# Attention and mixture-of-experts layer: another order for the first units of a step (output projection before the second maxima, two maxima before the second half of the weighted sums)

## The reference

```
scores = einsum('bhqd,bhkd->bhqk', q, k) * (1.0 / sqrt(HD))
attn   = softmax(scores * causal - (1.0 - causal) * NEG)
out    = einsum('bhqk,bhkd->bhqd', attn, v) -> b, t, d
a      = layernorm(out @ w_proj + b_proj + xn) * ln_gamma + ln_beta
f      = sum over the top 2 experts e of prob_e * (gelu(xn @ W1[e] + b1[e]) @ W2[e] + b2[e])
result = x + a + f
```

## Time and profile before

| | us |
|---|---|
| median of 3 runs (835.06 to 838.79) | 837.65 |
| the profiled execution, its own time | 838.32 |
| its span, first to last instruction | 836.6 |
| TensorE busy | 698.7 (84%) |
| VectorE busy | 653.4 (78%) |
| GpSimd busy | 557.4 (67%) |
| ScalarE busy | 544.8 (65%) |

### The profile page before, as it was taken

How to read it: one execution, slowest core, us unless ns; L and a number is a source line. 1 busy time by engine, 2 the same in 40 slices (tenths; PEclk the granted TensorE clock), 3 DMA queues, 4 the chain that set the end, 5 groups by cost and what they waited for, 6 DMA issues and landing times.

```text
span 836.6 us, 25028 instructions
## 1 busy us (share of the span) xinstructions
PE 698.7 (84%) x7876; PEld 518.2 (62%) x7878; DVE 653.4 (78%) x1550; ACT 544.8 (65%) x1107; POOL 557.4 (67%) x611
## 2 busy tenths in 40 slices
PE   2766989999999999999988878659999999999800
PEld 1543556666666666666656555338988889888700
DVE  5877978888978787878888887637878888888644
ACT  4812646666666666666756656538989999999700
POOL 8521758888877777777887786616766677667700
PEclk9987989999999999999999999869999999999955
DMA  9691323232322232223243333102222222222189
GB/s 271 230 312 59 94 68 100 89 102 89 101 90 100 91 100 91 99 92 107 84 148 120 111 107 93 28 14 73 87 83 80 86 87 82 86 77 90 49 277 333
DMA packets 113313, 93.66 MB, mean 112 GB/s; under 512 B 16618, under 2 KB 97650, under 8 KB 113268
## 3 DMA queue, kind: packets, MB, share of 16 engines
q1 hardware_dynamic: 95508, 70.26, 26.9%
q0 software_dynamic: 8704, 18.17, 6.1%
q10 hardware_dynamic: 9056, 4.66, 1.9%
HBM read 43.85 MB, written 48.93 MB: 111 GB/s over the span
## 4 chain that ended last, share of the span: by engine, by line
PE 60%; DVE 11%; ACT 7%; issue 7%; DMA 6%; POOL 6%; SPq 2%; ACTq 0%; POOLq 0%; DVEq 0%
PE wide L1323 11%; PE bank_head L1212 9%; PE bank_head L1314 5%; PE bank_maxB L1314 5%; PE wide L1177 5%; PE bank_maxA L1191 5%; DVE shift L966 4%; DMA xn_rows<-parts_dram 3%; PE bank_maxB L1191 3%; PE bank_maxA L1195 3%; PE wide L1181 3%; PE bank_misc L1237 3%; DMA pieces_f<-in_w 3%; POOL probs L601 2%; PE bank_maxB L1195 2%
## 5 line engine op out<-in xcount | busy, mean ns | idle before, releaser
L653 POOL DMA_INDIRECT parts_dram<-o_T,dest x144 | 161.3, 1120 | 75.9 <-issue 48.5
L601 POOL TENSOR_SCALAR_AFFINE_SELECT probs<-probs 128x512 f32<-128x512 f32 (+1 forms) x192 | 152.3, 805 | 83.1 <-ACT probs L687 81.0
L687 ACT ACTIVATE probs<-wide 128x1024 f32<-128x1024 f32 x192 | 185.4, 1023 | 31.1 <-PE wide L1177 18.9
L966 DVE TENSOR_REDUCE shift<-bank_maxA 128x2 f32<-128x512 f32 (+1 forms) x192 | 132.3, 689 | 52.4 <-PE bank_maxA L1195 48.7
L592 POOL DMA_INDIRECT x_slots<-xn_rows,slot_i x128 | 131.3, 1026 | 38.9 <-issue 37.5
L966 DVE TENSOR_REDUCE shift<-bank_maxB 128x2 f32<-128x512 f32 (+1 forms) x192 | 131.6, 685 | 5.4 <-PE bank_maxB L1195 1.3
L731 ACT ACTIVATE probs<-wide,b_all 128x256 f32<-128x256 f32 x288 | 121.5, 478 | 16.6 <-PE wide L1323 10.9
L1212 PE MATMUL bank_head<-probs,v_aug 128*32 128x256 f32 (+1 forms) x2048 | 99.6, 336 | 27.5 <-DVE x L992 22.9
L1323 PE MATMUL wide<-xgT_raw,xnT 128*128 128x256 f16 x864 | 109.3, 277 | 6.5 <-DVE xgT_raw L1073 6.5
L1212 PEld LDWEIGHTS bank_head<-probs,v_aug 128*32 128x32 f32 x2048 | 60.3, 112 | 72.3 <-issue 35.0
L1056 DVE TENSOR_TENSOR probs<-probs 128x512 f16<-128x512 f32 x144 | 99.7, 693 | 5.5 <-ACT probs L737 1.1
(11 more groups left out here) (178 smaller groups left out, 1253.3 us busy)
## 6 DMA issues: line engine op xcount, KB each, us to landing
qk_rows<-split SPq DMA_DIRECT2D x32, 512.0 KB, 3.0
x_slots<-fill SPq DMA_DIRECT2D x16, 598.5 KB, 7.8
fill<-x_slots SPq DMA_DIRECT2D x72, 133.0 KB
q_diag<-qk_rows SPq DMA_DIRECT2D x256, 32.0 KB, 1.8
k_cat<-qk_rows SPq DMA_DIRECT2D x64, 128.0 KB, 2.1
xn_rows<-parts_dram SPq DMA_DIRECT2D x8, 1024.0 KB, 11.7
x_all<-in_x SPq DMA_DIRECT2D x8, 512.0 KB, 7.5
pieces_f<-in_w SPq DMA_DIRECT2D x8, 512.0 KB, 4.0
```

What stands on the lines that cost most here:

```text
L601: pool.affine_select(out=part, in_=part, compare_op=ALU.is_ge, fill=0.0, base=0, pattern=[[0, n], [1, P]], channel_multiplier=-1).then_inc ...
L653: pool.indirect_dma_start(out=parts_dram, out_offset=bass.IndirectOffsetOnAxis(ap=dest[:, of, t:t + 1].bitcast(U32), axis=0), in_=y[:, of ...
L687: act.activation(probs[:, u, :], ps[:, :], ACT.Exp, scale=SCALE).then_inc(empty, 1)
L966: V.tensor_reduce(dst, ps[:, :].rearrange("p (j k) -> p j k", j=nh), axis=AX.X, op=ALU.max, negate=True).then_inc(empty, 1)
```

## The change

Two moves in the list USES. The row of proj goes one place forward, ahead of m1. The rows of m2 and m3 go ahead of o1. The order of units within each buffer stays as it was.

```diff
         USES = [
-            ("maxA", "m0", MAXIMA), ("maxB", "m1", MAXIMA), ("head", "proj", LAST),
+            ("maxA", "m0", MAXIMA), ("head", "proj", LAST), ("maxB", "m1", MAXIMA),
             ("misc", "qk", PROJECT),
-            ("head", "o1", FINISH), ("maxA", "m2", MAXIMA), ("maxB", "m3", MAXIMA),
+            ("maxA", "m2", MAXIMA), ("maxB", "m3", MAXIMA), ("head", "o1", FINISH),
             ("misc", "v", MAXIMA), ("maxA", "m4", MAXIMA), ("wide0", "s0", SOFT),
```

## The result

The changed kernel takes 858.26 us (median of 4 runs, 856.63 to 859.95) where the kernel before, run beside it, takes 836.44 us: a ratio of 1.0255, 95% interval 1.0229 to 1.0282. It is slower by some 22 us. The profiled execution of the changed kernel took 856.63 us (its span is 854.9 us, that of before 836.6), so the two traces that are compared here differ by 18.3 us.

A forecast was written before the change was run, and what follows sets the result against it. TensorE was taken to bound the loop, busy 13.38 of 14.00 us a step. Loop 13.0 and tail 3.3 us on the profiled 838.32 made 854.6 us, or 854 against the median; range 846 to 861.

The forecast's parts named there:

- The walk through a loop step: One loop step followed in the new order on the old clock: 0.43 to 0.81 us longer, 0.65 taken.
- the long v: TensorE's v ahead of m4 taken at its full 0.50 us instead of 0.34, so m4 starts at 309.82.
- (b): VectorE in the loop: addition and statistics go ahead of the maximum of m1; maxB is released 1.6 to 1.8 us later.
- (c): TensorE in the loop: m3, now ahead of o1, waits for maxB; TensorE idles about 1.1 us with o1 behind.
- The loop term: Loop steps 4 to 23: 20 x 0.65 = 13.0 us longer, bounds 8.6 and 16.2.
- step (e): Written-out steps 24 to 32: two pay 0.65 us in full, seven 0.28 each; together 3.3 us, bounds 0.9 and 5.9.
- The rival that was priced at 2%: TensorE's clock falls from 2.4 to 1.2 GHz; paid in nine tail steps, 13 us more, 867; chance 0.02.
- o1 did not fill m3's gap: Rival on TensorE in the loop: o1 runs while m3 waits, -0.3 us a step, about 831; chance 0.03.
- the larger loss: Loop: ScalarE's copy of o1 keeps its 0.6 us lag, exponentials start late; up to 0.4 us a step, 861; chance 0.08.
- VectorE's statistics did not shrink: Rival in the loop: VectorE's 1.51 us between addition and split shrinks below 0.6, m1's maximum not late; about 823; chance 0.02.
- nothing hid the loss: Rival in the loop: ScalarE or GpSimd already sets the step's length, so no change; 838 to 842; chance 0.04.

The follow-up runs named there:

- e3: Changed kernel with TensorE keeping the changed list and VectorE given the old order (maximum of m1 ahead of addition and statistics): 835.35 us.
- e4: Kernel before with TensorE's old list kept, VectorE alone taking the addition and statistics ahead of the maximum of m1: 834.25 us.
- e5: Changed kernel with the maximum of m1 put between addition and statistics on VectorE, TensorE's order unchanged: 833.41 us.
- e7: Kernel before with VectorE's split of a piece of expert weights (line 1035) done twice in a row in the written-out steps: 847.42 us.
- e9: Changed kernel with VectorE's split of a piece of expert weights moved from ahead of the addition to behind the maximum of m5: 854.27 us.
- e2: Kernel before with only the second move, m2 and m3 ahead of o1, the projection staying behind m1: 830.11 us.
- e1: Kernel before with only the first move, the projection ahead of m1 on TensorE and VectorE, o1 staying ahead of m2 and m3: 833.17 us.
- e10: e2 with VectorE's split of a piece of expert weights moved behind the maximum of m5: 835.29 us.
- e6: Changed kernel with VectorE's split of a piece moved from ahead of the addition to the end of the step in which ScalarE rounded it: 853.56 us.
- e8: e2 with VectorE's split of a piece moved to the end of the step in which ScalarE rounded it: 834.76 us.

## Why the prediction was right, and where it was not

**The walk through a loop step held at every point.** Measured from the end of m0's mask (304.28 in the earlier trace rows, 311.04 in the changed kernel):

| | forecast | measured |
|---|---|---|
| addition starts | 0.69 to 0.91 | 0.89 |
| maximum of m1 over | 2.88 to 3.10 | 2.98 |
| m3 starts | 2.94 to 3.16 | 3.04 |
| m4 starts | 5.16 to 5.38 (5.54 with the long v) | 5.37 |

m4 stood at 4.73 before, so the step loses 0.64 us there, and 0.62 from start to start (14.62 against 14.00); 0.65 was taken. That no later work gives it back held too. That the cause is the one of steps (b) and (c) is shown by e3, e4 and e5: without the statistics ahead of the maximum, or with o1 ahead of m3, nothing is lost.

**The loop term** was 13.0 us and came out at 11.4 between the two traces. Of these, steps 6 to 23 give 11.6 us; steps 4 and 5 give nothing: they take 19.21 and 14.70 us in the changed kernel, 19.45 and 14.68 in the kernel before. It is not shown that the order costs nothing there, since in both traces a stretch at half clock stands in step 4. The kernel before has one from 106.0 to 112.9 us, the changed kernel from 108.2 to 111.6. e7, whose loop is that of the kernel before, waits just as long in step 4 and has no such stretch:

```profile
107.31 2.79 PE L1212 MATMUL bank_head<-probs,v_aug 128*32 128x256 f32 x32 [3.57 <-DVE x L992]
```

```profile
106.55 1.51 PE L1215 MATMUL bank_head<-probs,v_aug 128*32 128x256 f32 x32 [3.58 <-DVE x L993]
```

(The kernel before, then e7. The 3.57 us are the longest wait in the earlier trace rows.) In e7 steps 4 and 5 take 17.01 and 14.21 us, and against e7's loop, 283.2 us, the changed one is 13.9 us longer. So the forecast lies between what two executions of the old loop give, and the term is right within what step 4 does by itself; that "20 x 0.65" came so near is owed in part to chance.

**The tail term, step (e), was mis-sized: 3.3 us with bounds of 0.9 and 5.9, measured 9.2.** Step by step, with the steps that have a half-clock stretch in the changed kernel in bold:

| step | 24 | 25 | 26 | 27 | 28 | 29 | 30 | 31 | 32 |
|---|---|---|---|---|---|---|---|---|---|
| before | 14.43 | 14.85 | 15.42 | 15.64 | 15.48 | 15.77 | 16.62 | 14.85 | 15.87 |
| after | 14.58 | 15.67 | 15.66 | **17.13** | **17.14** | **17.29** | **17.12** | 15.52 | 18.02 |

Where neither half clock nor a long transfer came in, the steps went about as forecast: 25 and 31, the two in which the chain was to go through TensorE, pay 0.82 and 0.67 us (0.65 forecast), 24 and 26 pay 0.15 and 0.24 (0.28 forecast). The two things that step (e) did not have are the rest.

The four steps with a stretch pay 5.2 us. What a stretch costs can be read in three ways: 1.38 us in e7; 1.55 us in the changed kernel itself, whose four steps with one take 17.17 us in the mean and steps 25, 26 and 31, with the same wait and none, 15.62; and 0.92 us against e9, where steps 28 to 30 have no stretch, but wait for ScalarE instead (16.26 us in the mean against 17.18). By these the four stretches are 3.7 to 6.2 us of the 9.2 (an estimate). Step 32 has 2.15 us, exactly what its piece's transfer took longer, 6.52 us against 4.37 in the kernel before. Why that one transfer took 6.52 us is open. In the other kernels a transfer that leads the chain takes 3.85 to 6.09 us, so it is not shown to come from the change.

Step (e) also took m3's wait as 2.2 us, where it is 1.88, and its upper bound reckons all nine steps at 0.65 us and not at the 0.81 of the walk. With that it would have been 7.3, which is too low as well.

**The rival that was priced at 2% is the one that came.** The clock did fall, as an addition to the forecast and not in its place. The argument against it was that a tail stretch with 3.25 us of idling in 16.00 kept 1.00. The sum of the idle time was the wrong measure: in the kernel before it lay in pieces of at most 1.42 us. The change did not add idle time to steps 27 to 30, where TensorE idles for 1.90 to 3.04 us before and 1.96 to 2.04 after; it put nearly all of it into one piece. The price, 1.4 us a step, was near e7's 1.38, but for four steps and not nine, and by luck: it was read from a stretch at 108 to 122 us of which 4.9 us ran at half clock, not 3.4.

**The other rivals.** o1 did not fill m3's gap: matmuls stayed in order. The lag of ScalarE's copy behind o1, from which the larger loss was reckoned, was 0.6 us before and is 0.07 now (o1 over at 316.13, copy at 316.20); that rival fell. (Its price should read 862, not 861: 854 and 8.) VectorE's statistics did not shrink, and nothing hid the loss.

**The total.** 854 was forecast, 858.26 measured. In this pair of traces the loop term was 1.6 us too high, the tail term 5.9 too low, and what lies outside steps 4 to 32 gave 2.3 us back. That errors of opposite sign met in the sum is luck; the mechanism of the loop is not. The other three runs of the changed kernel are 1.5 to 3.3 us above the profiled one, at a lower granted clock over the span (0.942 to 0.945 against 0.953); further stretches at half clock would do that, but these runs have no trace.

## What to carry to other kernels

Where one list sets the order of several engines, a row that is moved for one engine's sake moves on the others as well: walk each engine, and look for a release that comes later than the unit that waits for it in its new place. A unit that needs a buffer which is still being read belongs behind the units that are ready; here the half of the change that put ready units ahead of a waiting one won some 7 us (e2), and the other half, harmless by itself (e1), turned that into a loss of 22. In stretches where TensorE must wait anyway, look at the longest single idle time and not at the sum alone: here two or three short waits left the clock at full speed, and one of 1.88 us or more was often followed by half clock.

## What the runs showed of the hardware

**The clock.** Over the twelve kernels, between 380 and 520 us, 16 stretches at half clock were seen, each 3.4 us long, and each began within the last 0.7 us of an idle time of TensorE of 1.88 us or more, or up to 1.1 us behind it. Of 35 idle times of 1.0 to 1.87 us in that range none was followed by one. Of the 28 that were 1.88 us or longer 12 were not followed either, the longest of them 2.68 us (e7, steps 25, 26 and 29). In step 4, outside that range, TensorE idles for 2.33 to 3.58 us at one go in each of the twelve, and a stretch follows or overlaps in four; the longest, 3.58 us in e7, has none. So the length of an idle time alone does not decide it, and what else does is open.

**The split of a piece beside GpSimd.** Line 1035 took 1.21 or 1.22 us in e2, e9 and e10, and 1.65 to 2.15 us in most steps of e6 and e8, where it stands beside GpSimd's masks (line 601) at the end of a step. What counts is which of the two came first. In all twelve traces, up to 545 us, a mask was already running at the split's start in 17 cases, and the split took 1.65 to 2.15 us; in 8 cases the mask came up during the split, which took 1.21 or 1.22 us, and the mask ended 0.49 to 0.96 us behind it. One case of each kind in e8, GpSimd's rows and then VectorE's, and a split of e10 with no mask near it:

```profile
422.58 1.80 POOL L601 TENSOR_SCALAR_AFFINE_SELECT probs<-probs 128x512 f32<-128x512 f32 x2
...
441.50 1.95 POOL L601 TENSOR_SCALAR_AFFINE_SELECT probs<-probs 128x1024 f32<-128x1024 f32 x1 [0.28 <-ACT probs L687]
```

```profile
423.33 2.13 DVE L1035 TENSOR_TENSOR xnT<-pieces_f,xnT 128x1024 f16<-128x1024 f32 x1
...
441.29 1.21 DVE L1035 TENSOR_TENSOR xnT<-pieces_f,xnT 128x1024 f16<-128x1024 f32 x1
```

```profile
432.82 1.22 DVE L1036 TENSOR_TENSOR xnT<-pieces_f,xnT 128x1024 f16<-128x1024 f32 x1
```

The first mask is over at 424.38, 1.05 us into the split, and the split takes 0.91 us longer. The Trainium skill (SBUF — State Buffer, SBUF: two separate sides) says that VectorE, in an operation with two inputs in SBUF such as this one, and GpSimd share a pair of ports, which the one that starts first holds for its whole instruction while the other is blocked. These rows agree with it; no run here varied the mask alone.
